# A skewed expert pipeline, maps made earlier and gathers issued ahead: one core of a Trainium2 chip

## The chip, the cores and the metric

The kernel runs on one core of one Trainium2 chip. The core has five engines that run side by side and meet through semaphores: TensorE (matrix products and transposes, called turns here), VectorE, ScalarE, GpSimd and SyncE. SyncE issues plain DMAs, GpSimd issues the DMAs whose rows are chosen by an index. The metric is the device time of one execution in microseconds.

## The reference, cut to what matters

One layer: attention over 1024 tokens of width 256, then a mixture of experts with a shared expert.

```python
def _gate(x, gate_w, gate_bias):
    scores = jax.nn.sigmoid(x @ gate_w.T)          # 32 experts, best 2 of 4 groups, best 4 experts
    ...
    return (topk_idx, topk_w * SCALE)

def _moe(x, topk_idx, topk_w, w1, w2, w3):
    flat_e = topk_idx.reshape(-1)
    oh = jax.nn.one_hot(flat_e, E, dtype=jnp.int32)
    pos = (jnp.cumsum(oh, axis=0) * oh).sum(-1) - 1
    keep = pos < CAP                               # CAP = 64 slots for each expert
    slot = jnp.where(keep, pos, CAP)
    buf = jnp.zeros((E, CAP, H), x.dtype).at[flat_e, slot].set(x_rep, mode='drop')
    h = jax.nn.silu(jnp.einsum('ech,ehf->ecf', buf, w1)) * jnp.einsum('ech,ehf->ecf', buf, w3)
    ob = jnp.einsum('ecf,efh->ech', h, w2)
    y = ob[flat_e, jnp.minimum(slot, CAP - 1)]
    y = jnp.where(keep[:, None], y, 0.0)
    return (y.reshape(n, K, H) * topk_w[:, :, None]).sum(1)
...
shared = jax.nn.silu(x @ shared_gate) * (x @ shared_up) @ shared_down
return (out + shared).reshape(b, s, h)
```

## The kernel before, in words

The tokens lie in 8 tiles of 128. Attention and routing come first. Routing ends in a table that says for each of 32 x 64 slots which token is in it; `slot_index` (line 1041) writes it as row numbers, `gather_idx` and `res_idx`. Two experts of 64 slots fill one tile of 128 partitions, a pair; two pairs make a group, so there are 16 pairs and 8 groups (`EGROUPS`).

For each group g the stage works like this:

- GpSimd gathers the token rows of its two pairs from HBM, one indirect DMA for each (line 500, `gather`).
- TensorE turns them (`turn_slots`, line 1622), four transposes of 128x128, into the first halves of banks 0 and 1, which every group uses. ScalarE (line 743) and VectorE (line 1155) each bring one bank to SBUF as `slotT`, scaled and shifted (`slot_evac`).
- TensorE multiplies with w1 and w3 (`expert_up`, line 1638), one call for each pair. ScalarE takes the silu (line 762), VectorE the product (`expert_hid`, line 1170).
- TensorE turns the hidden tile (`turn_hid`, line 1651), ScalarE copies it out (`hid_evac`, line 750), and TensorE multiplies with w2 (`expert_down`, line 1660).
- VectorE scales the result by the slots' scores (`expert_evac`, line 1181) into one of four buffers `ob`. GpSimd returns it to its rows in HBM with one indirect DMA for each pair (line 509, `give_back`), for the first 13 pairs (`BACK`).

A buffer `ob` is written again four groups later, after its returns have landed. The last three pairs don't go through HBM: their results are added by products with 0/1 maps of tokens by slots (`back_map`, line 1188, 16 instructions; `back_map_first`, line 1194, 8 instructions).

When all 13 returns have landed, SyncE loads the results of the 8 token tiles (lines 420 to 425). VectorE then adds them for the tiles, with TensorE's sums for the last three pairs (lines 1244 to 1262), and SyncE stores each tile.

Every engine runs its instructions in the order in which the code writes them; no scheduler moves anything. So the order around the change is in the loops: the loop over g on TensorE, on ScalarE and on VectorE, and the loop on GpSimd with `AHEAD = 6`. In the loop before, TensorE does the first pair's `expert_up`, then the hidden turn of the group before, the slot turn of the next group, the second pair's `expert_up`, and `expert_down` of the group before. The shared expert's products (`shared_down`, line 1295 in the trace) lie between the first groups and behind the last; VectorE multiplies its hidden tiles (`shared_hid`, line 1058) and adds its results to `base` (`shared_add`, line 1063).

In the trace, names that differ by their number are merged: `bank` is any of banks 4 to 7, `score_pair` holds banks 0 to 3, `arena` holds the gathered rows, `slotT` and three of the `ob` buffers, `aT` the fourth, `h2T` the expert stage's hidden tiles, `prob` their transposes, `w_sb` any of the weights.

## Time and profile before

| | |
|---|---|
| median of 3 runs | 151.42 us (151.39 to 151.52) |
| span of the profiled execution | 161.2 us, 2747 instructions |
| TensorE busy | 145.7 us (90%) |
| VectorE busy | 111.7 us (69%) |
| ScalarE busy | 65.0 us (40%) |
| GpSimd busy | 48.5 us (30%) |
| DMA | 31.28 MB, mean 194 GB/s |

For the profiled execution the span from its first to its last instruction is given, and no time of its own beside it. The timed runs are executions of their own, without the profiler. Busy time is the time in which an engine works on an instruction. TensorE's ends are modelled, so 90% says little of how full it is. A number in brackets in a row of the timeline is the time the engine stood idle ahead of the row, and what released it: "issue" is nothing that the profile shows, "remote" another core or a queue that the profile doesn't know. The page gives the whole span in 40 slices of 4.03 us:

```profile
PE   7889799999999999999999999717997989699992
DVE  2848989898986497798759824107672949559994
ACT  3233680486155428749879411101232323131000
POOL 7400004279520000002000077773176536500000
PEclk9999999999999999999999999995699999999999
```

The expert stage runs from about 92 to 143 us.

### The profile page before, as it was taken

Reading aid. Unit: us, or ns where it says so; the run is one execution under the profiler, and the core shown is the slowest. Engines: PE = TensorE matmul, PEld = TensorE weight load, DVE = VectorE, ACT = ScalarE, POOL = GpSimd, SP = SyncE. Lnnn points to the kernel's source line nnn. Section 1 sums busy time; section 2 is a strip of 40 time slices with the busy share of each in tenths; the row PEclk is TensorE's granted clock in tenths of the full one; section 3 lists DMA queues with packets and bytes.
Section 4 is the critical chain, followed back from the end, with each engine's and each line's share of the span. In section 5 each row is a group of like instructions: output and inputs, shape, how many; then the busy total and the mean of one; then the engine's idle time right before and its main releaser. Section 6 shows DMA issues by size and latency. Waiting matters only on the chain.

```text
span 161.2 us, 2747 instructions
## 1 busy us (share of the span) xinstructions
PE 145.7 (90%) x915; PEld 105.2 (65%) x915; DVE 111.7 (69%) x394; ACT 65.0 (40%) x173; POOL 48.5 (30%) x71
## 2 busy tenths in 40 slices
PE   7889799999999999999999999717997989699992
PEld 7846548468566775898787887404564555368881
DVE  2848989898986497798759824107672949559994
ACT  3233680486155428749879411101232323131000
POOL 7400004279520000002000077773176536500000
PEclk9999999999999999999999999995699999999999
DMA  4999999999999997001003034543014011159983
GB/s 114 277 385 387 418 418 375 349 348 348 352 348 350 347 349 242 1 28 51 0 5 109 2 76 117 116 116 94 0 47 105 33 48 45 47 151 343 406 283 134
DMA packets 22080, 31.28 MB, mean 194 GB/s; under 512 B 2065, under 2 KB 18231, under 8 KB 22066
## 3 DMA queue, kind: packets, MB, share of 16 engines
q1 hardware_dynamic: 20642, 27.71, 50.6%
q0 software_dynamic: 1424, 3.39, 7.8%
q8 instruction: 7, 0.11, 0.3%
q14 instruction: 7, 0.06, 0.1%
HBM read 23.65 MB, written 8.13 MB: 197 GB/s over the span
## 4 chain that ended last, share of the span: by engine, by line
PE 51%; DVE 26%; issue 7%; another core or an unknown queue 5%; DMA 4%; ACT 4%; SPq 1%; DVEq 0%
PE bank L1638 8%; PE bank L1445 7%; PE score_pair L1497 5%; PE bank L1660 4%; PE score_pair L1423 4%; PE score_pair L1419 4%; DMA w_sb<-in_L_wmod_dram 4%; PE bank L1497 3%; PE bank L1432 2%; PE score_pair L1445 2%; DVE base L1262 2%; PE score_pair L1651 2%; DVE aT L853 2%; PE score_pair L1295 2%
## 5 line engine op out<-in xcount | busy, mean ns | idle before, releaser
L1638 PE MATMUL bank<-w_sb,arena 128*64 128x256 f32 x128 | 18.3, 408 | 1.3 <-issue 1.2
L500 POOL DMA_INDIRECT arena<-token_rows,gather_idx x16 | 16.1, 1009 | 10.3 <-DVE gather_idx L1046 5.8
L509 POOL DMA_INDIRECT results<-arena,res_idx x11 | 11.0, 999 | 13.3 <-DVE arena L1181 10.9
L1445 PE MATMUL bank<-arena 128*128 128x256 f32 x56 | 13.7, 382 | 0.2 <-ACT arena L602 0.2
L1638 PEld LDWEIGHTS bank<-w_sb,arena 128*64 128x64 f32 x128 | 9.0, 145 | 7.5 <-issue 5.2
L473 POOL TENSOR_TENSOR base<-aT,mod 128x256 f32<-128x256 f32 x8 | 5.8, 726 | 24.3 <-DVE aT L857 20.6
L1445 PEld LDWEIGHTS bank<-arena 128*128 128x128 f32 x56 | 10.1, 190 | 2.3 <-issue 1.3
L593 ACT ACTIVATE prob<-score_pair,nmax 128x128 f32<-128x128 f32 (+7 forms) x8 | 5.9, 742 | 11.6 <-DVE nmax L930 11.5
L1651 PE MATMUL score_pair<-ident,h2T 128*128 128x128 f32 x16 | 3.7, 319 | 7.5 <-DVE base L1063 4.3
L1423 PE MATMUL score_pair<-arena 128*128 128x512 f32 (+3 forms) x24 | 10.1, 504 | 0.0
L1419 PE MATMUL score_pair<-arena 128*128 128x512 f32 (+3 forms) x24 | 9.8, 490 | 0.0
L750 ACT COPY prob<-score_pair 128x256 f32<-128x256 f32 x8 | 3.0, 372 | 16.3 <-PE score_pair L1651 9.9
L1660 PE MATMUL bank<-w_sb,prob 128*64 128x256 f32 x64 | 9.2, 412 | 0.0
L1651 PEld LDWEIGHTS score_pair<-ident,h2T 128*128 128x128 f32 x16 | 1.7, 149 | 10.9 <-issue 7.5
L743 ACT ACTIVATE arena<-score_pair,modc 128x256 f32<-128x256 f32 x8 | 4.5, 565 | 10.3 <-issue 5.0
L1155 DVE TENSOR_SCALAR arena<-score_pair,modc 128x256 f32<-128x256 f32 x8 | 4.3, 542 | 6.2 <-remote 4.4
L488 POOL DMA_INDIRECT first_row<-results,first_idx x1 | 1.2, 1247 | 23.6 <-DVE rows L956 23.6
L1170 DVE TENSOR_TENSOR h2T<-h2T,bank 128x256 f32<-128x256 f32 x8 | 3.3, 418 | 6.7 <-ACT h2T L762 3.7
L629 ACT ACTIVATE h2T<-bank,modc 128x128 f32<-128x128 f32 x16 | 6.3, 449 | 4.0 <-PE bank L1453 3.9
L1295 PE MATMUL score_pair<-arena,w_sb 128*128 128x512 f32 x16 | 7.3, 597 | 0.3 <-issue 0.3
L1295 PE MATMUL bank<-arena 128*128 128x256 f32 x32 | 7.5, 382 | 0.0
L1308 PE MATMUL score_pair<-ones_bf 128*128 128x128 bf16 x72 | 6.5, 278 | 1.1 <-POOL ones_bf L433 1.1
(223 smaller groups left out, 345.4 us busy)
## 6 DMA issues: line engine op xcount, KB each, us to landing
w_sb<-in_L_ffn_w_dram SPq DMA_DIRECT2D x12, 1024.0 KB, 12.5
results<-prob SPq DMA_DIRECT2D x1, 4096.0 KB, 15.8
w_sb<-results SPq DMA_DIRECT2D x6, 512.0 KB, 7.9
token_rows<-rows SPq DMA_DIRECT2D x8, 144.0 KB
xin<-in_L_attn_x_dram SPq DMA_DIRECT2D x4, 256.0 KB, 6.4
w_sb<-in_L_wmod_dram SPq DMA_DIRECT2D x1, 1024.0 KB, 9.5
out_dram<-base SPq DMA_DIRECT2D x8, 128.0 KB, 2.3
w_sb<-in_L_attn_qkv_dram SPq DMA_DIRECT2D x1, 768.0 KB, 7.6
```

Of the source, the lines that this page charges most:

```text
L500: nc.gpsimd.indirect_dma_start(out=slot_in[:, r, :], out_offset=None, in_=rows_d, in_offset=bass.IndirectOffsetOnAxis(ap=gather_idx[:, r:r ...
L509: nc.gpsimd.indirect_dma_start(out=results_d, out_offset=bass.IndirectOffsetOnAxis(ap=res_idx[:, r:r + 1], axis=0), in_=ob[g % 4][:, (r % ...
L629: last = a.activation(h2T[:, k, P * i:P * i + P], ring_bank(f"x{i}")[:, P * k:P * k + P], ACT.Identity, bias=modc[:, 1, k:k + 1], scale=mo ...
L1295: last = t.matmul(dst, lhsT, rhs, start=(n == 0), stop=(n == len(terms) - 1))
L1308: t.matmul(bank[1][:, 0:P], ones_bf[:, :], ones_bf[:, :], start=True, stop=True)
L1419: t.matmul(dst[:, 0:w], qT[:, 0, P * i:P * i + P], xnT[:, 0, 512 * b:512 * b + w], start=True, stop=False)
L1423: last = t.matmul(dst[:, 0:w], qT[:, 1, P * i:P * i + P], xnT[:, 1, 512 * b:512 * b + w], start=False, stop=True)
L1445: last = t.matmul(PV_BANK[i][:, 0:H], probT[:, i % 2, j, :], vo[:, j, :], start=(j == 0), stop=(j == i))
L1497: last = t.matmul(SH_BANK[key][:, 256 * c:256 * c + 256], w[:, k, P * ft:P * ft + P], h2T[:, k, 512 * half + 256 * c:512 * half + 256 * c ...
L1638: last = t.matmul(bank[4 + g % 2][CAP * side:CAP * side + CAP, 2 * F * r:2 * F * r + 2 * F], slotT[:, k, CAP * e:CAP * e + CAP], w13_sb[:, ...
L1651: last = t.transpose(bank[2 + g % 2][:, P * r:P * r + P], hid[:, g % 2, r, :], ident[:, :])
L1660: last = t.matmul(bank[6 + g % 2][CAP * side:CAP * side + CAP, H * r:H * r + H], hidT[:, g % 2, r, CAP * side:CAP * side + CAP], w2_sb[:, ...
```

## The change

It has five parts.

1. TensorE's loop is skewed by one more group: in iteration g it does both halves of `expert_up(g)`, the slot turn of group g + 2, `expert_down(g - 2)` and the hidden turn of group g - 1. Two slot turns precede the loop. Behind the loop `expert_down` of groups 5 and 6 follow each other.
2. ScalarE's and VectorE's loops follow that order.
3. VectorE makes the 16 `back_map` instructions ahead of its loop, between the last steps of the shared expert, and the 8 `back_map_first` in iteration 1. Before, they came two tiles at a time in iterations 1 to 4 and four in 5 and 6.
4. `back_first` lies in `xin` and not in a weight tile any more.
5. GpSimd issues all 16 gathers and then the 13 returns. Before, the gathers of group 7 came behind the first two returns.

```diff
-        back_first = w13_sb[:, 16].rearrange("p w k f -> p (w k f)").bitcast(BF16).rearrange("p (t q) -> p t q", t=NT)
+        back_first = xin[:, 6:8, :].rearrange("p a b -> p (a b)").bitcast(BF16).rearrange("p (t q) -> p t q", t=NT)
...
-            AHEAD = 6
             for g in range(EGROUPS):
                 gather(g)
-                if g == AHEAD:
-                    pool.wait_ge(ridx_done, 1)
-                if g >= AHEAD:
-                    give_back(g - AHEAD)
-            for g in range(EGROUPS - AHEAD, (BACK + 1) // 2):
+            pool.wait_ge(ridx_done, 1)
+            for g in range((BACK + 1) // 2):
                 give_back(g)
...
-            slot_evac(0)
-            for g in range(EGROUPS):
-                if g >= 1:
-                    hid_evac(g - 1)
-                if g + 1 < EGROUPS:
-                    slot_evac(g + 1)
+            def expert_silu(g):
                 act.wait_ge(up_mm, g + 1)
...
+            slot_evac(0)
+            slot_evac(1)
+            for g in range(EGROUPS - 1):
+                expert_silu(g)
+                if g + 2 < EGROUPS:
+                    slot_evac(g + 2)
+                if g >= 1:
+                    hid_evac(g - 1)
+            hid_evac(EGROUPS - 2)
+            expert_silu(EGROUPS - 1)
...
-            shared_hid(1, 0)
-            shared_hid(1, 1)
-            shared_add(0)
...
+            settle()
+            shared_hid(1, 0)
+            for i in range(0, 2):
+                back_map(i)
+            shared_hid(1, 1)
+            for i in range(2, 4):
+                back_map(i)
+            shared_add(0)
             slot_evac(0)
+            for i in range(4, 6):
+                back_map(i)
+            slot_evac(1)
+            for i in range(6, NT):
+                back_map(i)
             for g in range(EGROUPS - 1):
-                slot_evac(g + 1)
+                expert_hid(g)
                 if g == 0:
                     shared_add(1)
-                expert_hid(g)
-                scores_of_slots(g)
+                if g + 2 < EGROUPS:
+                    slot_evac(g + 2)
+                if g >= 2:
+                    expert_evac(g - 2)
                 if g == 0:
                     score_sums()
-                else:
-                    expert_evac(g - 1)
-                if 1 <= g < 5:
-                    back_map(2 * g - 2)
-                    back_map(2 * g - 1)
-                elif g >= 5:
-                    for i in range(4 * g - 20, 4 * g - 16):
+                elif g == 1:
+                    for i in range(NT):
                         back_map_first(i)
-            scores_of_slots(EGROUPS - 1)
+                if g == 0:
+                    scores_of_slots(0)
+                scores_of_slots(g + 1)
+            expert_evac(EGROUPS - 3)
             expert_evac(EGROUPS - 2)
             expert_hid(EGROUPS - 1)
...
             turn_slots(0)
             shared_down(1, (0,))
+            turn_slots(1)
             for g in range(EGROUPS - 1):
                 expert_up(g, 0)
+                expert_up(g, 1)
+                if g == 0:
+                    shared_down(1, (1,))
+                if g + 2 < EGROUPS:
+                    turn_slots(g + 2)
+                if g >= 2:
+                    expert_down(g - 2)
                 if g >= 1:
                     turn_hid(g - 1)
-                turn_slots(g + 1)
-                expert_up(g, 1)
-                if g >= 1:
-                    expert_down(g - 1)
-                else:
-                    shared_down(1, (1,))
             last_g = EGROUPS - 1
+            expert_up(last_g, 0)
             turn_hid(last_g - 1)
-            expert_up(last_g, 0)
+            expert_down(last_g - 2)
             expert_down(last_g - 1)
             expert_up(last_g, 1)
```

The instructions of an engine stand in these rows in program order, with the line first; the changed kernel's lines lie 12 higher on TensorE. First TensorE, before, from the slot turn of group 0 to the first layer of group 2 (1622 turns slots, 1638 is the first layer, 1651 turns the hidden tile, 1660 is the second layer, 1295 the shared expert; `w13_sb` and `w2_sb` are the experts' weights, `score_pair0` holds banks 0 and 1):

```order
L1622 MATMUL score_pair0<-ident,arena 128x128 x4
L1295 MATMUL score_pair1<-shd_sb,aT 128x256 x2
L1638 MATMUL bank4<-w13_sb,arena 64x256 x4
L1622 MATMUL score_pair0<-ident,arena 128x128 x4
L1638 MATMUL bank4<-w13_sb,arena 64x256 x4
L1295 MATMUL score_pair1<-shd_sb,aT 128x256 x2
L1638 MATMUL bank5<-w13_sb,arena 64x256 x4
L1651 MATMUL score_pair1<-ident,h2T 128x128 x2
L1622 MATMUL score_pair0<-ident,arena 128x128 x4
L1638 MATMUL bank5<-w13_sb,arena 64x256 x4
L1660 MATMUL bank6<-w2_sb,prob 64x256 x4
L1638 MATMUL bank4<-w13_sb,arena 64x256 x4
```

And in the changed kernel, the same piece (1634, 1650, 1663, 1672 and 1307 are these lines there):

```order
L1634 MATMUL score_pair0<-ident,arena 128x128 x4
L1307 MATMUL score_pair1<-shd_sb,aT 128x256 x2
L1634 MATMUL score_pair0<-ident,arena 128x128 x4
L1650 MATMUL bank4<-w13_sb,arena 64x256 x8
L1307 MATMUL score_pair1<-shd_sb,aT 128x256 x2
L1634 MATMUL score_pair0<-ident,arena 128x128 x4
L1650 MATMUL bank5<-w13_sb,arena 64x256 x8
L1634 MATMUL score_pair0<-ident,arena 128x128 x4
L1663 MATMUL score_pair1<-ident,h2T 128x128 x2
L1650 MATMUL bank4<-w13_sb,arena 64x256 x8
```

The first layer's two halves stand together (x8), group 1's slots are turned ahead of it, and the hidden turn of group 0 comes behind group 1's whole first layer and group 3's slot turn. Then TensorE at the end of the stage, before, from the slot turn of group 7:

```order
L1622 MATMUL score_pair0<-ident,arena 128x128 x4
L1638 MATMUL bank4<-w13_sb,arena 64x256 x4
L1660 MATMUL bank7<-w2_sb,prob 64x256 x4
L1651 MATMUL score_pair1<-ident,h2T 128x128 x2
L1638 MATMUL bank5<-w13_sb,arena 64x256 x4
L1660 MATMUL bank6<-w2_sb,prob 64x256 x4
L1638 MATMUL bank5<-w13_sb,arena 64x256 x4
```

In the changed kernel, from the slot turn of group 7, which comes one group earlier:

```order
L1634 MATMUL score_pair0<-ident,arena 128x128 x4
L1672 MATMUL bank7<-w2_sb,prob 64x256 x4
L1663 MATMUL score_pair1<-ident,h2T 128x128 x2
L1650 MATMUL bank4<-w13_sb,arena 64x256 x8
L1672 MATMUL bank6<-w2_sb,prob 64x256 x4
L1663 MATMUL score_pair1<-ident,h2T 128x128 x2
L1650 MATMUL bank5<-w13_sb,arena 64x256 x4
L1663 MATMUL score_pair1<-ident,h2T 128x128 x2
L1672 MATMUL bank7<-w2_sb,prob 64x256 x4
L1672 MATMUL bank6<-w2_sb,prob 64x256 x4
L1650 MATMUL bank5<-w13_sb,arena 64x256 x4
```

A hidden turn stands alone between products now, and the second layers of groups 5 and 6 stand together (banks 7 and 6) instead of each behind a half of a first layer. Last, GpSimd, before:

```order
L500 DMA arena<-token_rows,gather_idx 128x288 x14
L509 DMA results<-arena,res_idx 4096x256 x2
L500 DMA arena<-token_rows,gather_idx 128x288 x2
L509 DMA results<-arena,res_idx 4096x256 x4
L509 DMA results<-aT,res_idx 4096x256 x2
L509 DMA results<-arena,res_idx 4096x256 x5
```

In the changed kernel:

```order
L500 DMA arena<-token_rows,gather_idx 128x288 x16
L509 DMA results<-arena,res_idx 4096x256 x6
L509 DMA results<-aT,res_idx 4096x256 x2
L509 DMA results<-arena,res_idx 4096x256 x5
```

The two gathers from behind the first two returns stand ahead of them.

## Rows read from the trace of the kernel before

**Rows 1.** The page's first line
```profile
span 161.2 us, 2747 instructions
```

**Rows 2.** Timeline, 96 to 109: start, us, engine, line, operation [idle before]
```profile
96.24 1.89 PE L1295 MATMUL bank<-shd_sb,aT 128*128 128x256 f32 x8
...
96.51 0.69 DVE L1058 TENSOR_TENSOR aT<-prob,score_pair 128x512 f32<-128x512 f32 x1 [1.04 <-issue]
...
98.17 0.69 DVE L1063 TENSOR_TENSOR base<-bank,base 128x512 f32<-128x512 f32 x1 [0.97 <-issue]
...
100.47 0.66 PE L1622 MATMUL score_pair<-ident,arena 128*128 128x128 f32 x4
...
102.07 1.13 PE L1295 MATMUL score_pair<-shd_sb,aT 128*128 128x256 f32 x4
...
103.71 0.54 DVE L1155 TENSOR_SCALAR arena<-score_pair,modc 128x256 f32<-128x256 f32 x1 [4.40 <-remote]
...
108.73 0.69 DVE L1063 TENSOR_TENSOR base<-score_pair,base 128x512 f32<-128x512 f32 x1 [4.48 <-remote]
```

**Rows 3.** Windows, 110 to 113: us, busy by engine, then PEclk, DMA share, GB/s
```profile
110.00:113.00 3.00, 3.00 (x14) 1.90 (x15) 1.79 (x6) 0.65 (x2) 0.33 (x1) 0.50 0.28 76
```

**Rows 4.** Timeline of TensorE in the expert groups
```profile
99.45 1.08 PE L1638 MATMUL bank<-w_sb,arena 128*64 128x256 f32 x8
...
115.96 0.44 PE L1651 MATMUL score_pair<-ident,h2T 128*128 128x128 f32 x2
...
118.54 1.03 PE L1638 MATMUL bank<-w_sb,arena 128*64 128x256 f32 x8
119.50 0.44 PE L1651 MATMUL score_pair<-ident,h2T 128*128 128x128 f32 x2
119.78 0.60 PE L1622 MATMUL score_pair<-ident,arena 128*128 128x128 f32 x4
120.31 1.08 PE L1638 MATMUL bank<-w_sb,arena 128*64 128x256 f32 x8
121.22 1.03 PE L1660 MATMUL bank<-w_sb,prob 128*64 128x256 f32 x8
...
132.39 0.44 PE L1651 MATMUL score_pair<-ident,h2T 128*128 128x128 f32 x2 [0.58 <-DVE h2T L1170]
...
135.23 0.44 PE L1651 MATMUL score_pair<-ident,h2T 128*128 128x128 f32 x2
135.60 1.08 PE L1638 MATMUL bank<-w_sb,arena 128*64 128x256 f32 x8
```

**Rows 5.** GpSimd's timeline, and line 509's durations in ns, min/median/max
```profile
92.39 1.00 POOL L500 DMA_INDIRECT arena<-token_rows,gather_idx  x1 [5.75 <-DVE gather_idx L1046]
...
109.33 1.00 POOL L500 DMA_INDIRECT arena<-token_rows,gather_idx  x1 [0.30 <-issue]
...
120.34 1.11 POOL L500 DMA_INDIRECT arena<-token_rows,gather_idx  x1 [0.30 <-issue]
...
128.54 0.98 POOL L509 DMA_INDIRECT results<-aT,res_idx  x1 [0.53 <-issue]
...
139.25 0.98 POOL L509 DMA_INDIRECT results<-arena,res_idx  x1 [0.65 <-DVE arena L1181]
...
L509 POOL DMA_INDIRECT results<-arena,res_idx x11: 982/986/1075, 116.3 to 139.2; - x11
```

**Rows 6.** Timeline of VectorE, two batches of maps
```profile
119.89 0.87 DVE L1188 TENSOR_SCALAR xin<-count_f,slot_token 128x128 bf16<-128x128 f32 x4
...
128.57 1.00 DVE L1188 TENSOR_SCALAR xin<-count_f,slot_token 128x128 bf16<-128x128 f32 x4
```

**Rows 7.** Timeline of SyncE and VectorE, the start of the close
```profile
141.80 0.32 SPq L422 DMA_DIRECT2D w_sb<-results  x1
...
138.49 0.88 DVE L1181 SCALAR_TENSOR_TENSOR arena<-bank,slot_score,mod 128x256 f32<-128x256 f32 x2 [0.90 <-PE bank L1660]
...
146.77 0.48 DVE L1244 SCALAR_TENSOR_TENSOR base<-w_sb,scale,base 128x256 f32<-128x256 f32 x1
```


## The prediction

> **What bounds the kernel now.** I first set the span against the timed runs. The profiled execution spans 161.2 us [rows 1]; the runs shown have a median of 151.42 us, and no run is shorter than the span inside it. So at least 9.8 us of this trace are not in the timed runs, and before any sum I have to find which. Next I read the timeline from 96 to 109 us, since the list of waits names a "remote" releaser only there [rows 2]. TensorE's turn of group 1's slots starts at 100.47 and takes 0.66, yet VectorE, idle, starts to read it at 103.71. The shared expert's product runs from 102.07 to 103.20, yet VectorE, idle again, adds it at 108.73. The work was done and its answer came 2.6 and 5.5 us late. Earlier the same kind of answer comes at once: a product of 96.24 ends at 98.13, and VectorE adds at 98.17 [rows 2]. The two holes in VectorE are 4.40 and 4.48 us, and they lie in the chain of waits. Behind them TensorE had stood idle, and its granted clock was 0.50 from 110 to 113 us [rows 3], the lower of its two levels, 1.2 GHz. Two holes of 8.9 us and a slow stretch are about the surplus.
>
> I therefore take the lateness as a thing of the profiled execution and lay out the expert stage without it, from row durations. Then another engine comes forward. GpSimd issues 16 gathers and 13 returns, 29 in all. A gather takes 1.00 and the next starts 1.30 after it: the 13 steps from 92.39 to 109.33 are 1.303 each; a return takes 0.98 to 1.07, with the same 0.30 ahead of it where it doesn't wait [rows 5]. If GpSimd never waits, its last return starts at 92.39 + 28 x 1.303 = 128.87, not at 139.25 [rows 5]. What follows the last return is fixed: SyncE's first load of results comes 2.55 later (141.80), VectorE's closing adds 4.97 after that (146.77) [rows 7]. A last return at 128.87 is 10.4 earlier than in the trace, and 161.2 - 10.4 = 150.8 leaves 0.6 for what lies around the span. So GpSimd's chain of issues bounds a timed run.
>
> VectorE's maps may stretch that chain. Beside a batch of four that had started first, an issue took 1.11 instead of 1.00; where the issue started first, it kept its 0.98 and the four maps took 1.00 instead of 0.87 [rows 5, 6]. There are six such batches (16 and 8 instructions) in either kernel, so the toll lies between 0 and 0.6; I take 0.3 and put the last return at 129.2. The Trainium skill says (SBUF — State Buffer, SBUF: two separate sides) that a VectorE instruction in a two-port mode keeps GpSimd from writing descriptors. The trace agrees that the two exclude each other. By the rule's full length 24 maps of some 0.28 would cost 6.7 us, in both kernels alike; the rows show 0.1 for four, and the sum goes by them.
>
> **Does TensorE keep up, before?** I sum from 99.45, the first start of the experts' first layer [rows 4]. Occupancies at full clock, start to start [rows 4]: half a first layer 0.91, and 0.96 when a turn follows; a slot turn 0.53 before products; a hidden turn 0.28 before a slot turn and 0.37 before products (135.23 to 135.60). A whole group is 119.50 - 115.96 = 3.54, which leaves 0.86 for its second layer. The first part, 0.96 + 0.53 + 0.91 + 0.96 (shared product) + 0.96, leads to 103.8; the first hidden turn waits for VectorE's addition and product and starts near 104.2. Five periods make 121.9. The last has no half of a first layer in it, 2.84 (135.23 - 132.39): 124.7. Then 0.37 and 0.91 put group 6's second layer at 126.0. It takes 1.03, and GpSimd starts 0.76 after VectorE's scaling begins (138.49 to 139.25) [rows 5, 7]: the last return could start at 127.8. GpSimd is free for it at 129.2. TensorE has 1.4 us in hand.
>
> **The change, part by part.**
> Gathers: group 7's two issues go ahead of the first two returns. There are still 29, and group 7's slot turn, due after 118, waits for them in neither order. GpSimd's long wait for its first return is not in the timed runs either way, since group 0's results are there before 110. The first return now starts at 92.39 + 16 x 1.303 = 113.2. SyncE's queue has nothing between its stores of rows and the loads of results. VectorE waits for the return of group 0 before it scales group 4; it lands some 4 us after 113.2, and that scaling is due at 124. Cost nothing.
> Maps: all 24 still run while GpSimd issues, so the toll stays. The first two batches, 0.87 each, fill gaps of 1.04 and 0.97 ahead of two shared products on VectorE [rows 2, 6]. The third stands between two slot evacuations and delays the second to 100.7, for a first layer that starts at 103.3. Nothing, with a bound of 0.2 for TensorE should one be late; ScalarE's new order is as far from its needs. Moving the map from w_sb to xin changes no duration.
> Skew: per group TensorE now does the first layer's two halves, slot turn, second layer, hidden turn. The work is the same, but the turns don't stand side by side any more, so that it goes between products and turns four times in a group instead of twice. From the rows: 0.91 + 0.96 + 0.53 + 0.96 + 0.37 = 3.73 against 3.54. The trace shows no second layer with turns on both sides; the bounds are no extra at all (3.54) and twice the extra (3.92), and 3.73 is the sum of its nearest rows.
> New sum: slot turn of group 1 at 99.45, 0.53; first layer 1.87; shared product 0.96; slot turn 0.53; first layer 1.87; slot turn 0.44 (a turn follows it), hidden turn 0.37; first layer 1.87; slot turn 0.53: group 0's second layer starts at 108.4. Three periods: group 3's at 119.6. Without a slot turn 3.20: group 4's at 122.8. Then 0.96, hidden turn 0.37, half a first layer 0.96, hidden turn 0.37: group 5's at 125.5. No hidden tile is waited for: between asking and needing stand a first half more than before.
> The end: the second layers of groups 5 and 6 now stand together, and three returns wait behind them. Group 5's first could start at 125.5 + 1.03 + 0.76 = 127.3. GpSimd is free for it at 92.39 + 26 x 1.303 + 0.3 = 126.6. It waits 0.7, and the last return follows two steps later, at 129.9 against 129.2. VectorE's other way to the closing adds, by group 7, ends near 135.2 (before 134.9); by the returns these start at 129.9 + 2.55 + 4.97 = 137.4, so that way hides.
> **Forecast:** 151.42 + 0.7 = 152.1 us. A toll of 0.6 makes the difference 0.4, none 1.0; with no extra for the turns it is 0, with twice the extra 1.6.
>
> **Rivals.**
> No change: GpSimd's chain ends at 129.2 in both, because TensorE needs 0.7 less than I sum over 26 us. For it: the price of a break is read from gaps of 0.05 to 0.15 us. Against: these gaps stand in every group. 151.4 us.
> Faster: the late answers are in the timed runs too. Then TensorE waits in both kernels, and the new order puts half a first layer and more between asking and needing: for the loop at the start, 0.53 + 1.87 = 2.4 us, less six times 0.19: 1.3 gained, 150.1 us. For it: the lateness is in the trace. Against: 9.8 us of the span would need another home, and I find none. By the Trainium skill (Runtime: NRT & Kernel Launch, The ~15µs preamble/postamble breakdown) some 6.2 us of a profile's total lie outside the execution. Were they in this span, only 3.6 of the 9.8 us would be lateness that timed runs lack, and this rival would hold at its 150.1; no row here shows such a piece inside the span.
> Slower by more: GpSimd is quicker without the profiler, so that TensorE bounds both. Before, the last return then follows group 6's second layer at 127.8; after, it is the third behind group 5's, 127.3 + 2.6 = 129.9. That is 2.1 more, 153.5 us. It decides fully once GpSimd's step falls under 1.25 us. Against it: 1.30 stands in thirteen steps.
>
> **How the numbers follow.** About 0.2%, 0.3 us, is what a measurement of this kernel tells from no change. Forecast case (0.3 to 1.6 slower): 0.37. Slower by more: 0.10. No change: 0.31. Faster: 0.22. So 0.22 faster, 0.31 the same, 0.47 slower. The forecast's own range is 151.8 to 153.0. For 8 in 10 the range takes in no change, the faster case down to 150.3, and the worst up to 153.2.
>
> **What would show it.** In the changed kernel's profile: GpSimd steps of 1.30 over all 16 gathers; issues of up to 1.11 beside maps near 95 to 102; 3.7 us, not 3.5, from one hidden turn to the next at full clock; the last three returns 1.3 apart, the first of them behind VectorE's scaling of group 5. If "remote" holes are there again, they should be shorter, and the profiled span can fall by more than the timed runs do. I am wrong if the timed runs gain more than 0.3 us, or if hidden turns stand 3.5 apart, or if the last three returns stand apart, each behind a scaling of its own.

## The result, and the profile after

The changed kernel takes 153.7 us (median of 4 runs, 153.2 to 153.84) where the kernel before takes 151.47 (151.39 to 151.63): 1.0125 times as long, interval 1.0083 to 1.0166. By the medians it is slower by 2.2 us, by the ratio by 1.9 (1.3 to 2.5). In every ratio here executions more than 1.5% above the fastest of their kernel are left out, and in no median. The forecast was slower by 0.7, at 152.1, with a range to 153.2: the sign was right, the size was not. The profiled execution of the changed kernel spans 151.4 us and took 153.2, so 1.8 us lie around a span.

GpSimd's timeline of the changed kernel (start, us, engine, line, operation, idle before and what ended it), first gather to last return:

```profile
91.41 1.00 POOL L500 DMA_INDIRECT arena<-token_rows,gather_idx  x1 [5.75 <-DVE gather_idx L1048]
...
96.62 1.05 POOL L500 DMA_INDIRECT arena<-token_rows,gather_idx  x1 [0.30 <-issue]
...
103.19 1.23 POOL L500 DMA_INDIRECT arena<-token_rows,gather_idx  x1 [0.30 <-issue]
...
112.57 1.03 POOL L509 DMA_INDIRECT results<-arena,res_idx  x1 [0.30 <-issue]
...
121.16 0.98 POOL L509 DMA_INDIRECT results<-aT,res_idx  x1 [1.13 <-DVE aT L1180]
...
124.27 0.99 POOL L509 DMA_INDIRECT results<-arena,res_idx  x1 [0.85 <-DVE arena L1180]
...
127.03 0.98 POOL L509 DMA_INDIRECT results<-arena,res_idx  x1 [0.49 <-DVE arena L1180]
...
129.61 0.98 POOL L509 DMA_INDIRECT results<-arena,res_idx  x1 [0.30 <-issue]
```

These answer to [rows 5]. The usual idle time ahead of an issue is 0.30, so GpSimd waited 0.83 us for group 3's rows, 0.55 for group 4's and 0.19 for group 5's, 1.57 in all. From the first gather to the last return it took 129.61 - 91.41 = 38.20 us. Two gathers took longer than 1.00: 1.05 beside a batch of maps (96.62), and 1.23 (103.19) beside VectorE's sums of the scores (`score_sums`), not beside maps.

TensorE in the same execution, to be held against [rows 4]: the turn of group 1's slots, the first layer of group 2 and the turn of group 4's slots with its weight load (PEld) behind it, group 0's second layer, one whole group, and the second layers of groups 5 and 6:

```profile
98.47 0.63 PE L1634 MATMUL score_pair<-ident,arena 128*128 128x128 f32 x4
...
105.09 1.95 PE L1650 MATMUL bank<-w_sb,arena 128*64 128x256 f32 x16
...
107.14 0.66 PE L1634 MATMUL score_pair<-ident,arena 128*128 128x128 f32 x4
107.14 0.42 PEld L1634 LDWEIGHTS score_pair<-ident,arena 128*128 128x128 f32 x4 [0.56 <-DMA arena<-token_rows,gather_idx]
...
107.72 1.08 PE L1672 MATMUL bank<-w_sb,prob 128*64 128x256 f32 x8
...
112.59 0.44 PE L1663 MATMUL score_pair<-ident,h2T 128*128 128x128 f32 x2
112.96 1.95 PE L1650 MATMUL bank<-w_sb,arena 128*64 128x256 f32 x16
114.84 0.66 PE L1634 MATMUL score_pair<-ident,arena 128*128 128x128 f32 x4
115.42 1.08 PE L1672 MATMUL bank<-w_sb,prob 128*64 128x256 f32 x8
116.44 0.44 PE L1663 MATMUL score_pair<-ident,h2T 128*128 128x128 f32 x2
...
125.14 1.95 PE L1672 MATMUL bank<-w_sb,prob 128*64 128x256 f32 x16
```

From hidden turn to hidden turn it is 3.85 us (112.59 to 116.44): 0.37 to the first layer, 1.88 for it, 0.58 for the slot turn, 1.02 for the second layer. No product's or turn's row from 98 to 129 us has an idle time of its own, but one hides a wait: the turn of group 4's slots starts 2.05 us behind the first layer ahead of it (105.09 to 107.14), where 1.88 is usual. Its weight load waited for the gather issued at 103.19, which landed after 3.91 us, and the chain of waits runs through it. So up to 107.1 us GpSimd's gathers set the pace, and from there TensorE does, 0.17 us late; then GpSimd waits for TensorE.

In VectorE's timeline the first maps stand where they were meant to, and each shared product still starts within 0.23 us of TensorE's answer:

```profile
94.43 0.87 DVE L1187 TENSOR_SCALAR xin<-count_f,slot_token 128x128 bf16<-128x128 f32 x4
95.53 0.69 DVE L1060 TENSOR_TENSOR aT<-prob,score_pair 128x512 f32<-128x512 f32 x1 [0.23 <-PE score_pair L1509]
96.13 0.87 DVE L1187 TENSOR_SCALAR xin<-count_f,slot_token 128x128 bf16<-128x128 f32 x4
97.18 0.69 DVE L1065 TENSOR_TENSOR base<-bank,base 128x512 f32<-128x512 f32 x1 [0.18 <-PE bank L1307]
```

There is no "remote" hole anywhere in the profile. The close starts as [rows 7] had it: SyncE's first load stands 2.56 us behind the last return.

```profile
132.17 0.32 SPq L422 DMA_DIRECT2D w_sb<-results  x1
```

### The profile page after: what moved, and what is told of

The parts are those of the page before. It is cut to its first block, busy times and chain, and to the rows that moved or that the text cites. A ratio compares the mean times of both kernels' runs of the same rounds, so it can differ in the third digit from the quotient of the medians.

```text
span 151.4 us, 2747 instructions
## 1 busy us (share of the span) xinstructions
PE 143.9 (95%) x915; PEld 103.2 (68%) x915; DVE 112.3 (74%) x394; ACT 65.1 (43%) x173; POOL 48.5 (32%) x71
## 3 DMA queue, kind: packets, MB, share of 16 engines
q0 software_dynamic: 1424, 3.39, 8.4%
## 4 chain that ended last, share of the span: by engine, by line
PE 50%; DVE 17%; DMA 13%; POOL 7%; issue 6%; ACT 2%; SPq 2%; POOLq 1%; DVEq 0%
PE bank L1457 7%; POOL arena L500 6%; PE bank L1650 6%; PE score_pair L1509 5%; DMA w_sb<-in_L_attn_qkv_dram 5%; PE score_pair L1435 4%; PE score_pair L1431 4%; DMA w_sb<-results 4%; PE bank L1672 4%; DMA arena<-token_rows,gather_idx 3%; PE bank L1444 2%; PE bank L1307 2%; PE score_pair L1307 2%; PE score_pair L1457 2%; DVE base L1274 2%
## 5 line engine op out<-in xcount | busy, mean ns | idle before, releaser
L1650 PE MATMUL bank<-w_sb,arena 128*64 128x256 f32 x128 | 15.8, 385 | 0.0
L1650 PEld LDWEIGHTS bank<-w_sb,arena 128*64 128x64 f32 x128 | 8.5, 136 | 4.8 <-issue 1.3
L1672 PE MATMUL bank<-w_sb,prob 128*64 128x256 f32 x64 | 8.4, 389 | 0.0
L753 ACT ACTIVATE h2T<-bank 128x256 f32<-128x256 f32 x8 | 3.1, 384 | 12.4 <-PE bank L1650 12.4
L931 DVE TENSOR_REDUCE bmax<-score_pair 128x1 f32<-128x128 f32 (+7 forms) x8 | 6.0, 751 | 1.7 <-PE score_pair L1435 1.7
L1320 PEld LDWEIGHTS score_pair<-ones_bf 128*128 128x128 bf16 x72 | 6.3, 132 | 1.1 <-POOL ones_bf L433 1.1
L1180 DVE SCALAR_TENSOR_TENSOR arena<-bank,slot_score,mod 128x256 f32<-128x256 f32 x12 | 5.2, 478 | 2.3 <-PE bank L1672 2.2
```

The lines of the kernel that those rows point to most:

```text
L931: chain(v.tensor_reduce(bmax[:, i:i + 1], score_pair[i % 2][:, 0:n], AX_X, ALU.max))
L1320: t.matmul(bank[1][:, 0:P], ones_bf[:, :], ones_bf[:, :], start=True, stop=True)
L1650: last = t.matmul(bank[4 + g % 2][CAP * side:CAP * side + CAP, 2 * F * r:2 * F * r + 2 * F], slotT[:, k, CAP * e:CAP * e + CAP], w13_sb[:, ...
L1672: last = t.matmul(bank[6 + g % 2][CAP * side:CAP * side + CAP, H * r:H * r + H], hidT[:, g % 2, r, CAP * side:CAP * side + CAP], w2_sb[:, ...
```

## The experiments

Eleven kernels ran in three groups, each group beside runs of the kernel before on the same chip. "Way" below is the time from the start of the first gather to the start of the last return in a kernel's profile; "landing" is the last return's time from there to its landing, read from the chain of waits.

| Kernel | median, us | ratio to before (95%) | span | way | landing |
|---|---|---|---|---|---|
| before, again | 151.65 (10) | 0.9989 (0.9956 to 1.0023) | 149.7 | 36.56 | 2.64 |
| changed | 153.7 (4) | 1.0125 (1.0083 to 1.0166) | 151.4 | 38.20 | 2.42 |
| changed, again | 154.01 (6) | 1.0152 (1.0106 to 1.0199) | 152.6 | 38.93 | 2.43 |
| no skew | 151.64 (12) | 0.9992 (0.9963 to 1.0022) | 151.0 | 36.51 | 2.43 |
| old order of gathers | 154.42 (4) | 1.0148 (1.0071 to 1.0224) | 152.8 | 38.82 | 2.44 |
| other tail | 153.73 (4) | 1.0116 (1.0068 to 1.0163) | 152.1 | 38.32 | 2.57 |
| turns joined | 154.79 (6) | 1.0181 (1.0131 to 1.0231) | 154.9 | 37.63 | 4.19 |
| turns joined, other tail | 155.22 (4) | 1.0231 (1.0175 to 1.0286) | 152.7 | 37.66 | 4.53 |
| turns joined, packet moved (1) | 154.51 (6) | 1.0199 (1.0162 to 1.0236) | 152.0 | 37.18 | 4.25 |
| turns joined, packet moved (2) | 155.70 (6) | 1.0262 (1.0201 to 1.0324) | 153.3 | 37.78 | 4.18 |
| before, one issue more | 155.30 (6) | 1.0132 (1.0066 to 1.0199) | 154.5 | 38.05 | 3.93 |
| changed, one issue more | 153.76 (10) | 1.0102 (1.0064 to 1.0139) | 152.3 | 38.85 | 2.42 |

Two parts of a span lie outside way and landing and scatter by themselves: the first gather starts at 91.4 to 92.7 us in these profiles, and where the landing is 2.4 to 2.6 us the end comes 21.2 to 22.2 us behind the last return. So spans of single profiles are not compared to the tenth here, and ways are.

### The kernel before, once more

No edit. 

> The kernel before, unchanged, for a second profile. Theory: GpSimd's chain of 29 issues bounds it, 28 steps of 1.303 from the first gather to the last return, 36.5 us, as soon as the late answers of TensorE are absent; the profile then has a span near 149.7 and no remote waits in the expert stage. Rival: the late answers belong to this order of work; then the span is again near 161 with remote waits near 100 to 109. Timed: 151.4 to 151.6 either way.

Its span is 149.7, which is 151.47 less the 1.8 around a span. (The forecast's laying out without the late answers had 150.8, with 0.6 around it.) GpSimd's timeline in it:

```profile
91.95 1.00 POOL L500 DMA_INDIRECT arena<-token_rows,gather_idx  x1 [5.74 <-DVE gather_idx L1046]
...
103.69 1.00 POOL L500 DMA_INDIRECT arena<-token_rows,gather_idx  x1 [0.30 <-issue]
...
125.90 1.01 POOL L509 DMA_INDIRECT results<-arena,res_idx  x1 [0.30 <-DVE arena L1181]
...
128.51 1.19 POOL L509 DMA_INDIRECT results<-arena,res_idx  x1 [0.30 <-issue]
```

No issue in between has more than 0.31 idle ahead of it. The way is 36.56 us against 28 x 1.303 = 36.48: GpSimd bounds this kernel, and its whole way is issues. The forecast's 36.8 is 0.25 too long. Part of that is the step: 16 gathers of 1.303 and 12 undisturbed returns of 1.29 make 36.33, so the stretches beside maps and elsewhere are some 0.2 us by this estimate, where the sum had 0.3.

How much TensorE has in hand can be read too. In the changed kernel, where GpSimd waits for a group's rows, it starts 0.76 us behind the start of VectorE's scaling (126.27 to 127.03), as the forecast had it. Here the scaling of group 5 starts at 124.79, so its return could start at 125.55, and it starts at 125.90:

```profile
124.79 0.88 DVE L1181 SCALAR_TENSOR_TENSOR arena<-bank,slot_score,mod 128x256 f32<-128x256 f32 x2
```

That leaves 0.35 us in hand at group 5, and 0.71 at group 6 (127.04 + 0.76 against 128.51). In the kernel without the skew it is 0.20 at group 5. The forecast's 1.4 looked at group 6 alone. One more row of TensorE matters below, the turn of group 4's slots. It stands 7.56 us behind the issue of the gather it reads (103.69), and in the changed kernel 3.95 (103.19 to 107.14):

```profile
111.25 0.60 PE L1622 MATMUL score_pair<-ident,arena 128*128 128x128 f32 x4
```

### Without the skew

The changed kernel's early maps and its sixteen gathers ahead, on TensorE's old order:

```diff
-            AHEAD = 6
             for g in range(EGROUPS):
                 gather(g)
-                if g == AHEAD:
-                    pool.wait_ge(ridx_done, 1)
-                if g >= AHEAD:
-                    give_back(g - AHEAD)
-            for g in range(EGROUPS - AHEAD, (BACK + 1) // 2):
+            pool.wait_ge(ridx_done, 1)
+            for g in range((BACK + 1) // 2):
                 give_back(g)
...
+            for i in range(0, 2):
+                back_map(i)
             shared_hid(1, 1)
+            for i in range(2, 4):
+                back_map(i)
```

> The changed kernel without its skew: all sixteen gathers ahead of the first return and the return's maps made early, as changed, but TensorE's order of the kernel before (second layer one group behind the first). Theory A (the skew alone costs): GpSimd's 28 steps run without a wait, 28 x 1.303 = 36.5 us plus about 0.3 us for three issues that were stretched beside the early maps; span 149.7 to 150.2, time 151.5 to 152.0, the group period 3.54 us. Rival B (the early maps or the gathers ahead carry part of it): at least 0.6 us of waits of GpSimd for returns stay, time 152.5 to 153.7.

Theory A holds: 151.64 us, the same as before within 0.3%, and a way of 36.51. Rows of GpSimd, first gather and last return:

```profile
92.25 1.00 POOL L500 DMA_INDIRECT arena<-token_rows,gather_idx  x1 [5.75 <-DVE gather_idx L1042]
...
128.76 0.99 POOL L509 DMA_INDIRECT results<-arena,res_idx  x1 [0.30 <-issue]
```

So on TensorE's old order the early maps and the gathers ahead cost and bring nothing, as forecast, and the loss needs the skew. (The skew with the maps in their old places was not run.) The span of this one execution is 1.3 us longer than that of the kernel before, all but 0.3 of it behind the last return (22.2 us to the end against 21.2); the ten or more timed runs of each show no such difference.

### The old order of the gathers under the skew

```diff
+            AHEAD = 6
             for g in range(EGROUPS):
                 gather(g)
-            pool.wait_ge(ridx_done, 1)
-            for g in range((BACK + 1) // 2):
+                if g == AHEAD:
+                    pool.wait_ge(ridx_done, 1)
+                if g >= AHEAD:
+                    give_back(g - AHEAD)
+            for g in range(EGROUPS - AHEAD, (BACK + 1) // 2):
                 give_back(g)
```

> The changed kernel with the gathers of the last two groups issued in the order of before (two behind the first returns). The skew gives group 0's rows at about 110.1 us, when GpSimd would issue the first return at 109.9. Theory: the waits for groups 3 to 5 bound the last return, so nothing changes: 153.3 to 154.0. Rival: issuing all gathers ahead was worth the wait for the first group's rows, and the old order loses 0.3 us or more per later group: 154.3 or more.

The median of four, 154.42, is 0.4 above the changed kernel's beside it (154.01). That lies in the rival's band, but the ratios are 1.0148 and 1.0152 and their intervals overlap widely: a difference under some 1 us four runs can't show. In its profile GpSimd waits 0.75 us more than usual at the first return, and then at groups 3, 4 and 5 as the changed kernel does (1.05, 0.78, 0.84 and 0.48 idle). The rival's 0.3 per later group doesn't show. The way, 38.82, is longer than the first changed profile's because a slot turn waited 0.71 us for its gather, of which more below. Issuing all gathers ahead takes away the wait at the first return, and the later waits hide that one anyway.

### One GpSimd issue more, in either kernel

```diff
+                if g == 4:
+                    nc.gpsimd.indirect_dma_start(
+                        out=half_v[:, 0, :], out_offset=None, in_=results_d.rearrange("r (a c) -> (r a) c", c=8),
+                        in_offset=bass.IndirectOffsetOnAxis(ap=first_idx[:, 0:1], axis=0),
+                        bounds_check=last_row, oob_is_err=False).then_inc(first_gathered, 16)
...
-            pool.wait_ge(ridx_done, 1)
+            pool.wait_ge(ridx_done, 1); pool.wait_ge(first_gathered, 32)
```

> The kernel before with one further small indirect DMA of 1.25 us on GpSimd behind the gathers of group 4, into an unused tile. Theory (GpSimd's chain bounds the kernel before): the time rises by the issue's whole step, 1.55 us, to 153.0. Rival (TensorE bounds both kernels): it rises by 0.2 at most, to 151.7.

> The changed kernel with the same further indirect DMA. Theory (in the changed kernel GpSimd waits 1.57 us in all for TensorE's results, 0.83, 0.55 and 0.19 beyond its step): the issue goes into those waits and the time stays at 153.5 to 153.9. Rival (GpSimd's chain bounds both kernels): 153.7 + 1.55 = 155.2.

An issue is the probe for an engine that bounds. Before: the way grows from 36.56 to 38.05, by 1.49. That is the issue's whole step of 1.30, and 0.19 more ahead of the last return, where the return before it took 1.19 us. No issue waits. The time grows by 2.0 us by the ratio (1.0 to 3.0), part of which is a late landing (below). Changed: the way is 38.85, within the 38.20 to 38.93 of the two profiles of the changed kernel, and the time stays, 153.76 against 153.7 and 154.01. GpSimd's chain no longer bounds the kernel, in the direct sense that one more issue is free. That also answers the rival "slower by more": TensorE bounds the kernel after but not before.

### Another tail

```diff
-            expert_up(last_g, 0)
-            turn_hid(last_g - 1)
             expert_down(last_g - 2)
+            turn_hid(last_g - 1)
+            expert_up(last_g, 0)
             expert_down(last_g - 1)
```

> The changed kernel with another order in TensorE's last groups: the second layer of group 5 and group 6's hidden turn ahead of group 7's first pair, so that group 5's rows are ready about 1 us earlier. Rival B (group 5's late second layer sets the last return, as the forecast had it): GpSimd's wait ahead of group 5's returns (0.49 us idle before it, 0.19 beyond the usual 0.30) goes and the time falls by the 0.7 us that the forecast laid on it, to about 153.0. Theory A (worked out from the changed kernel's profile): group 4's rows are ready at 124.27 us and four steps of 1.29 end at 129.43, against 129.61 now; the returns were held by group 3 and 4 first, so the gain is 0.2 us at most, time 153.4 to 153.7.

No gain: 153.73, and a way of 38.32, with one slot turn 0.41 us late for its gather. GpSimd no longer waits for group 5 and the last return comes where group 4 lets it. In its timeline, group 4's first return and the last return:

```profile
125.48 0.98 POOL L509 DMA_INDIRECT results<-arena,res_idx  x1 [0.84 <-DVE arena L1180]
...
130.63 1.13 POOL L509 DMA_INDIRECT results<-arena,res_idx  x1 [0.30 <-issue]
```

From 125.48 four steps of 1.29 give 130.64. In the changed kernel group 4's return would by itself have put the last one at 124.27 + 4 x 1.29 = 129.43, and group 5's wait put it at 129.61. So the bunch of the last three returns, on which the forecast laid its whole 0.7, is worth 0.2.

### The turns joined again

The hidden turn of a group goes back beside the slot turn, with the skew kept:

```diff
-                if g >= 2:
-                    expert_down(g - 2)
                 if g >= 1:
                     turn_hid(g - 1)
+                if g >= 2:
+                    expert_down(g - 2)
```

> The changed kernel with the hidden turn moved ahead of the second layer, so that it stands beside the slot turn again. Theory (the two further breaks per group cost 0.31 us, 3.85 against 3.54): TensorE's period is 3.54 to 3.6 from hidden turn to hidden turn, group 5's second layer comes some 1.7 earlier, and the time falls from 153.7 to 151.4 to 152.0. Rival (the second layers of groups 5 and 6 standing together, or the gathers and maps in front, cost the 2.2 us): it falls by 0.4 at most, to 153.3 or more.

TensorE's timeline, one group:

```profile
111.50 0.65 PE L1634 MATMUL score_pair<-ident,arena 128*128 128x128 f32 x4
112.00 0.38 PE L1663 MATMUL score_pair<-ident,h2T 128*128 128x128 f32 x2
112.31 1.08 PE L1672 MATMUL bank<-w_sb,prob 128*64 128x256 f32 x8
113.22 1.90 PE L1650 MATMUL bank<-w_sb,arena 128*64 128x256 f32 x16
115.05 0.66 PE L1634 MATMUL score_pair<-ident,arena 128*128 128x128 f32 x4
115.54 0.38 PE L1663 MATMUL score_pair<-ident,h2T 128*128 128x128 f32 x2
```

The price of the breaks is shown: 3.54 (112.00 to 115.54) with the turns side by side, 3.85 with them apart, the same instructions. But the way only falls from 38.20 to 37.63, not to 36.5, and the time doesn't fall at all. Two things were not foreseen. The first is in GpSimd's waits: 0.58 for group 3 and 0.54 for group 4 are left. Part of that comes from a slot turn which waited 0.29 us for its gather. In a later variant of this kernel (packet moved, 1), where no turn waits, the way is 37.18 and GpSimd still waits 0.44 us at group 4. So some 0.6 us over the 36.5 are left when neither the breaks nor a gather cost anything: 0.44 of waiting and 0.2 of stretched issues. That the waiting comes from each group's second layer standing behind another first layer is argued, not shown.

The second thing is behind the last return. The chain of waits (start, us, what) of this kernel and of the changed one:

```profile
129.56 4.19 DMA results<-arena,res_idx
```
```profile
129.61 2.42 DMA results<-arena,res_idx
```

The last return is issued at the same time and lands 1.8 us later. The DMA view of 131.6 to 133.3 us of the joined kernel (40 slices of 0.0425 us; then a queue's packets, MB, and share of 16 engines' time) shows what stood ahead of its last packets:

```profile
GB/s 0 386 0 0 0 0 0 0 0 0 0 0 0 0 0 0 0 0 0 0 0 0 96 0 0 0 0 0 0 0 0 0 96 0 0 0 0 0 0 0
q8 instruction: 1, 0.02, 3.2%
q0 software_dynamic: 5, 0.01, 2.8%
```

At 131.68 one instruction packet of 16 KB starts. Its share of 3.2% of 16 engines over 1.7 us is 0.87 us, so it ends near 132.55, and there, in the 23rd slice, a 4 KB packet of the return starts, the second of two at 132.97. All other packets of the return had started before 131.5. In the changed kernel the same view has the instruction packet first at 131.62, 0.1 us behind the start of the return's last packet, and nothing of the return after it but its counts:

```profile
GB/s 386 0 0 0 0 0 0 0 0 0 0 0 0 0 0 0 0 0 0 0 0 0 0 0 0 0 0 0 0 0 0 0 0 0 0 0 145 0 0 48
q8 instruction: 1, 0.02, 3.5%
...
q0 software_dynamic: 6, 0.00, 0.2%
```

The Trainium skill (DMA: Bandwidth & Descriptors, Queues, rings and completion order) says that each DMA engine takes turns between its queues a whole packet at a time. The trace fits it, with 0.87 us for the packet that stood ahead.

The late landing starts the loads late (133.89 against 132.17), and TensorE waits for them. Its row, and the window of 142 to 148 us, whose third number from the end is the granted clock:

```profile
143.82 3.78 PE L1725 MATMUL bank<-w_sb,ident 128*128 128x256 f32 x8 [3.19 <-DMA w_sb<-results]
```
```profile
142.00:148.00 6.00, 4.18 (x10) 3.38 (x11) 5.72 (x12) 0.00 (x0) 0.00 (x0) 0.58 0.98 380
```

In the changed kernel it waits 1.00 us there, keeps its full clock and does the same 8 products in 1.99:

```profile
142.01 1.99 PE L1725 MATMUL bank<-w_sb,ident 128*128 128x256 f32 x8 [1.00 <-DMA w_sb<-results]
```

So a landing 1.8 us late can cost twice: behind 3.19 us of idle time the granted clock was at its lower level, 1.2 GHz, for most of what followed. The timed runs of the joined kernel lie at 153.9 to 156.7 us, the longest being the profiled one with the low clock. No profile shows a joined kernel whose last return lands in time, so what its shorter way (37.18 to 37.78 in four profiles) would be worth then, some 0.4 to 1.0 us by the way alone, stays open.

### Both edits, and the packet moved

The joined kernel with the other tail:

> The kernel with the hidden turn moved next to the slot turn, and the tail's order of the run before. Theory A: group 4's rows (ready at 124.40 us there) bound the last return at 124.40 + 4 x 1.29 = 129.56 us as in the kernel without the tail's order; so no gain from the tail, span as that kernel's by the same landing of the last return. Rival B: group 5 bound it, and the last return is issued 0.7 us earlier or more.

Group 4 bounds again (124.10 us, then four steps to 129.26), no gain from the tail, as theory A had it; the landing is 4.53 here. The next two kernels are the joined one with waits that are satisfied already, early in the program, to move the packet:

```diff
+            for _ in range(20):
+                pe.wait_ge(consts, 1)
             pe.wait_ge(qkv_loaded, 16)
```
```diff
+                if first == 0:
+                    for _ in range(16):
+                        dve.wait_ge(cexp_done, 1)
                 dve.wait_ge(mod_mm, 1)
...
+            for _ in range(16):
+                act.wait_ge(c_loaded, 16)
```

> The kernel with the hidden turn moved next to the slot turn, and 20 more instructions in TensorE's stream: waits that are satisfied already, early in the program while TensorE waits for data. They move nothing else but the place in the program at which an instruction packet of 16 KB is fetched (at 131.6 us in that kernel's profile, on the DMA engine where the last two 4 KB packets of the last return then stood until 132.5 and 132.9, so that it landed 4.19 us after its issue instead of 2.42). Theory C (that collision made the joined kernel slow): the fetch comes 2 us or so earlier, the last return lands in 2.4 to 2.6 us, span 151.2 to 151.8, time 153.0 to 153.6. Rival D (something else makes the landing late): it stays near 4 us, time 154.4 to 155.0.

> The kernel with the hidden turn beside the slot turn, and 16 more waits (satisfied already) in VectorE's stream and 16 in ScalarE's, early in the program where both engines are idle. The 20 waits in TensorE's stream moved the late 16 KB instruction packet by 0.4 us against the last return only, and it still hit it. If the packet belongs to VectorE's or ScalarE's stream, it comes some us earlier now. Theory C (the packet's collision with the last return makes the joined kernel slow): if the packet starts more than 1 us ahead of the last return's packets or after them, the return lands 2.4 to 2.6 us after its issue, span 151.2 to 151.9, time 153.0 to 153.7. If the packet still stands among them, 3.9 to 4.5 us and 154.4 to 155.2. Rival D (the landing is late for another reason): 3.9 to 4.5 us wherever the packet is.

Neither got the packet out of the way: it started 1.68 and 1.73 us behind the last return's issue, among its packets, in place of 2.12. The return landed after 4.25 and 4.18 us, and the times are 154.5 and 155.7. As a test of theory C these two failed, because the case in which it differs from D didn't come about. What the twelve profiles of the table do show, read from the DMA records, is an order. In the five with a late landing of 3.93 to 4.53 us (four joined kernels, before with one issue more) the last one or two 4 KB packets of the return start behind the instruction packet, each time the first of them within 0.02 us of its end. In the seven others (both profiles of the changed kernel, before again, no skew, old order, other tail, changed with one issue more) the return's packets have all started before it, and the landing takes 2.42 to 2.64. That makes the collision likely. It doesn't decide it, since packets late for another reason would stand behind as well. And the packet's start alone doesn't part the cases: counted from the last return's issue it is 1.35 to 1.73 us in four late ones but 2.12 in the joined kernel, and 2.00 to 3.00 in the seven. Whose instructions it carries stays open: neither TensorE's nor VectorE's and ScalarE's extra instructions moved it as their number would have it.

### The changed kernel, once more

> The changed kernel as it is, on the chip of these comparisons. In its first profile the 16 KB packet started at 131.62 us, 0.1 us after the last of the return's 4 KB packets: a near miss. Theory: median 153.3 to 154.0, with spread, as the packet hits the last return in some executions; if this profile shows a hit, the last return lands about 1.7 us later. GpSimd's way from the first gather to the last return 38.0 to 38.4 us again.

Its median is 154.01. Both it and the way, 38.93, lie above the first profile's, and the rows of TensorE tell why:

```profile
99.58 0.66 PE L1634 MATMUL score_pair<-ident,arena 128*128 128x128 f32 x4 [0.19 <-DMA arena<-token_rows,gather_idx]
...
106.11 0.66 PE L1634 MATMUL score_pair<-ident,arena 128*128 128x128 f32 x4 [0.63 <-DMA arena<-token_rows,gather_idx]
```

The slot turns of groups 1 and 3 waited for their gathers, 0.82 us together; in the first profile these two did not, and that of group 4 waited 0.17. A gather lands 2.9 us after its issue at least, 3.3 in the median and 4.5 at most; in the first profile it was 2.8, 3.2 and 3.9.

The way is 0.73 us longer than in the first profile, and 0.82 - 0.17 = 0.65 of it are these waits. They are no accident of one profile. In eight of the nine profiles with the skew a slot turn of group 3 or 4 stands late behind a gather: by 0.17 and 0.82 us in the changed kernel, 0.71 in the old order, 0.41 with the other tail, 0.75 with one issue more, and 0.29, 0.43 and 0.54 in three of the joined ones. In the profiles without the skew (before again, no skew, before with one issue more) none does. The skew turns a group's slots one group earlier. In the kernel before, the turns of groups 2 to 4 start 5.7, 6.6 and 7.6 us behind the issue of their last gather; in the changed kernel those of groups 1 to 4 start 3.15 to 3.95 behind it, where a landing takes 2.8 to 4.5.

Which gather is late has a pattern too. In all nine profiles with the skew the longest landing, 3.77 to 4.55 us, is that of the gather behind whose issue, by 1.5 to 2.2 us, a 16 KB instruction packet starts (here at 103.74, behind the gather issued at 101.52). In the one joined kernel without a late turn, packet moved (1), that gather was group 3's first and not its last. That the packet is the cause is likely by the case above, not shown.

## Why the prediction was wrong in size

**The surplus of the profile: right.** The late answers were a thing of one profiled execution. Neither the second profile of before nor any of the changed kernel has a "remote" hole, and 149.7 + 1.8 = 151.5 closes the account of the kernel before. The rival "faster" had them in the timed runs and falls; 1.8 us around the span leave no room for a large piece of another kind.

**GpSimd bounds the kernel before: right**, with a way 0.25 too long: 36.8 with the maps' toll, and 36.56 measured. As the time before was given, this error of 0.25 goes straight into the difference: a way after of 37.5 would have been +0.9 and not +0.7. "TensorE has 1.4 us in hand" is wrong: at group 5, which that sum left out, it has 0.35, as VectorE starts the scaling 0.43 us behind the end of the second layer (124.36 to 124.79).

**The skew's period: the first step that failed.** The forecast summed 3.73 from "its nearest rows". Measured is 3.85, near its upper bound of 3.92. A slot turn between two products takes 0.58 (summed as 0.53), a second layer with turns on both sides 1.02 (summed as 0.96), the first layer 1.88 (1.87), the hidden turn 0.37 (0.37). Followed through the sum, from the first gather: the turn of group 1's slots +7.06, as summed; group 0's second layer +16.31 against +16.0; group 5's +33.73 against +33.1; its first return +35.62 against +34.9; the last return +38.20 against +37.5. Of the 0.7 that is missing 0.6 arises in TensorE's row of groups and 0.1 behind it. Of the 0.6, three periods of 3.85 are 0.36, and 0.17 is not work at all but the wait for group 4's gather. With the error in the way before, 38.20 - 36.56 = 1.64 stands in place of 0.7.

**A slot turn that waits for a gather was put at nothing: the second step that failed.** The forecast asked of the gathers only whether group 7's come in time. Groups 3 and 4 are the tight ones: with the skew their turns are due 3.7 to 3.8 us behind the issue of the last gather, and a landing took up to 4.55. In the five profiles with the skew and the turns apart the wait is 0.17 to 0.82 us, 0.57 in the mean. Their ways are 38.20 to 38.93, 38.62 in the mean, against 36.56 and 36.51: 2.1 us longer, which fits the measured loss (1.9 and 2.3 us by the ratios of the changed kernel's two sets of runs). As an estimate from these means, the 2.1 us are the 0.7 of the forecast, 0.25 by which the way before was too long, 0.55 by which TensorE's rows and what follows them were summed too short, and 0.6 of waits for gathers. Such ways scatter by up to 0.7 us from profile to profile, so the shares are rough.

**"The last three returns wait behind group 5": half right.** They are 1.3 apart behind group 5's scaling as forecast, but GpSimd had waited for groups 3 and 4 already, and with group 5's wait taken away (the other tail) the first profile's rows promise 0.2 and nothing was gained. The forecast looked for the wait at one place and put the whole price there.

**Gathers' order and maps at nothing: right on TensorE's old order.** The kernel without the skew takes 151.64 us. Under the skew the gathers' order made no difference that four runs could show; the maps were not tested under it.

**The rivals.** "No change" needed hidden turns 3.54 apart; they stand 3.85 apart. Even with them 3.54 apart the way stayed at 37.2 to 37.8: some 0.6 us over the 36.5 are left in the one profile without a wait for a gather, and 1.1 to 1.3 in those with one. "Slower by more" had the right size, 153.5, and the wrong ground: TensorE bounds both. It bounds only the kernel after, and there behind the gathers of groups 3 and 4; and GpSimd's step is still 1.30.

## What to carry to other kernels

Where two engines bound a stage within 1 us of each other, sum a new order on the second of them with the upper bounds of its gaps, and take its slack from every hand-over, not from the last one alone: here the last but one had half as much. Where a step is moved ahead, set its new start against the slowest landing of the transfer that it reads, and not against the median: here 3.7 us against 3.2 looks safe, and 4.5 isn't. Transposes stand side by side, and 64-column products too: each change between them costs some 0.05 to 0.15 us, and two more such changes cost 0.31 a group here. And one more issue of the engine that is thought to bound is a cheap probe of whether it does.

## What the runs showed of the hardware

- Instruction packets of 16 KB go through the DMA engines beside the data, 0.88 to 1.63 us each where they stood near the last return. In five of twelve profiles the last one or two 4 KB packets of a scatter started within 0.02 us of such a packet's end, and the whole transfer landed 1.3 to 2.1 us later than in the other seven. The five are the kernel before with one issue more and the four with the turns joined, so edits far from the last return went with it.
- Gathers of 128 rows landed 2.8 to 4.55 us after their issue, 3.1 to 3.3 in the middle. In the nine profiles with the skew the longest one was each time the gather with an instruction packet 1.5 to 2.2 us behind its issue.
- Behind TensorE's idle time in the close, the same eight products took 3.78 us at 3.19 (joined) and 3.06 us (before with one issue more), 3.47 and 3.39 at 1.97 and 2.00 us (packet moved), and 1.99 behind 1.00 (changed) but also behind 2.85 us (joined, other tail). The granted clock was at its lower level, 1.2 GHz, in the slow ones. The idle time just before doesn't decide it alone, and what else does was not found.
- An answer of TensorE's came 2.6 and 5.5 us late in one profiled execution and in none of the other twelve.
